# Between two transformer layers on one core: gated adds and residuals moved into TensorE's accumulators, row statistics read from PSUM, inverse roots by GpSimd's power

## What is computed

```python
h = layernorm(x) * (1 + ca) + sa
x = x + ga * L0_attn(h)            # adaptive window attention, 3 iterations, rows 0..308
h = layernorm(x) * (1 + cb) + sb
x = x + gb * L0_ffn(h)             # 8 experts, top 2 of softmax, gelu
h = layernorm(x) * (1 + ca1) + sa1
x = x + ga1 * L1_attn(h)           # W_in, complex decaying recurrence over tokens, W_out
h = layernorm(x) * (1 + cb1) + sb1
x = x + gb1 * L1_ffn(h)            # 8 experts, top 1, its own layernorm of h inside, relu
```

## Time and profile before

| | us |
|---|---|
| median of 3 runs | 447.66 (442.69 to 448.08) |
| profiled execution, span from first to last instruction | 450.3 |
| DVE busy in the span | 302.8 (67%) |
| PE busy | 299.0 (66%) |
| ACT busy | 171.9 (38%) |
| POOL busy | 171.5 (38%) |

### The profile page before, as it was taken

One profiled execution on the slowest core, in us unless ns is written; L12 is line 12 of the kernel. 1 busy time (PEld: TensorE's weight loads), 2 busy tenths in 40 slices (PEclk: granted clock), 3 DMA queues, 4 the chain that ended last, 5 costly groups with the idle time before them and its releaser, 6 DMA issues.

```text
span 450.3 us, 7419 instructions
## 1 busy us (share of the span) xinstructions
PE 299.0 (66%) x2070; PEld 218.3 (48%) x2071; DVE 302.8 (67%) x859; ACT 171.9 (38%) x331; POOL 171.5 (38%) x281
## 2 busy tenths in 40 slices
PE   2776888679916789786787999307616300599960
PEld 1662226333313232586687999303615300589960
DVE  7587975895779795288726666565988770277850
ACT  1144453216702157252515555747006600345520
POOL 9582870840166700002664455400000077044450
PEclk9885556555965557979989999856875555699995
DMA  2599700000011120011213221594000012323310
GB/s 78 97 366 362 229 3 0 1 1 1 8 47 41 53 32 0 1 34 51 60 48 72 64 66 38 157 307 146 1 1 1 0 59 106 97 69 81 97 48 0
DMA packets 37805, 32.93 MB, mean 73 GB/s; under 512 B 10765, under 2 KB 28770, under 8 KB 37776
## 3 DMA queue, kind: packets, MB, share of 16 engines
q1 hardware_dynamic: 33792, 25.10, 20.0%
q0 software_dynamic: 3936, 7.49, 5.3%
q10 hardware_dynamic: 48, 0.00, 0.0%
HBM read 19.50 MB, written 13.98 MB: 74 GB/s over the span
## 4 chain that ended last, share of the span: by engine, by line
PE 41%; DVE 30%; issue 10%; ACT 6%; POOL 5%; DMA 2%; DVEq 2%; SPq 1%; another core or an unknown queue 1%; POOLq 0%; ACTq 0%
PE ps L1237 9%; PE ps L1248 7%; PE ps L1058 6%; PE ps L1033 5%; PE ps L1053 5%; DVE mx L1765 4%; POOL rows L589 4%; DVE hb L1910 2%; DVE stats L1373 2%; PE ps L1009 2%; PE ps L1080 2%; ACT wide L782 2%; SPq L293 1%; POOL out L601 1%
## 5 line engine op out<-in xcount | busy, mean ns | idle before, releaser
L589 POOL DMA_INDIRECT rows<-token_rows,posu x48 | 49.1, 1024 | 115.1 <-DVE token_rows L1688 73.0
L601 POOL DMA_INDIRECT back<-ys,places x39 | 38.6, 990 | 81.9 <-DVE ys L1921 72.4
L1910 DVE TENSOR_TENSOR hb<-ps,b_in 128x512 f32<-128x512 f32 x62 | 42.5, 686 | 36.6 <-PE ps L1237 31.9
L1248 PE MATMUL ps<-w_out,hg 128*128 x496 | 66.3, 278 | 0.7 <-issue 0.7
L1248 PEld LDWEIGHTS ps<-w_out,hg 128*128 128x128 f32 x496 | 61.0, 194 | 1.1 <-issue 0.9
L871 ACT ACTIVATE hg<-hb 128x512 f32<-128x512 f32 x62 | 39.1, 630 | 36.4 <-DVE hb L1910 23.4
L1765 DVE TENSOR_REDUCE mx<-ps 128x2 f32<-128x512 f32 (+2 forms) x48 | 44.4, 948 | 7.2 <-PE ps L1033 6.6
L1237 PE MATMUL ps<-xsT,w_now 128*128 128x128 f32 x256 | 38.6, 299 | 10.8 <-DVE hb L1910 5.2
L1033 PE MATMUL ps<-feat,qs 64*128 64x281 bf16 (+2 forms) x128 | 33.3, 431 | 14.1 <-DVE mx L1765 10.0
L1237 PEld LDWEIGHTS ps<-xsT,w_now 128*128 128x128 f32 x256 | 34.6, 210 | 12.9 <-issue 8.4
L770 ACT COPY qs<-ps 128x768 bf16<-128x768 bf16 (+1 forms) x21 | 15.3, 728 | 64.4 <-PE ps L1009 38.8
(11 more groups left out here) (388 smaller groups left out, 549.6 us busy)
## 6 DMA issues: line engine op xcount, KB each, us to landing
rows<-blank SPq DMA_DIRECT2D x20, 260.0 KB, 7.3
xs<-rows SPq DMA_DIRECT2D x62, 64.0 KB
w_in<-in_L_ffn_w_fc SPq DMA_DIRECT2D x1, 2048.0 KB, 15.5
w_in<-in_L_ffn_W SPq DMA_DIRECT2D x1, 2048.0 KB, 10.2
rest<-rows SPq DMA_DIRECT2D x23, 65.0 KB
token_rows<-in_L_attn_x SPq DMA_DIRECT2D x1, 832.0 KB, 8.3
wmod<-in_L_wmod SPq DMA_DIRECT2D x2, 384.0 KB, 4.6
rows<-token_rows,posu POOLq DMA_INDIRECT x48
```

What stands on the lines that cost most here:

```text
L589: pool.indirect_dma_start(ROWS[l], bass.IndirectOffsetOnAxis(ap=posu[:, k, j:j + 1], axis=0), token_rows[:, j, 0:WIDTH[l]], None).then_inc ...
L601: pool.indirect_dma_start(where, bass.IndirectOffsetOnAxis(ap=target[r] if l else places[:, t, :].bitcast(U32)[:, 0:1], axis=0), ys[:, r, ...
L1248: mm = pe.matmul(ps[:, 6 + c % 2, 0:D], hg[:, c % RING, n * P:(n + 1) * P], w_out[:, bass.ds(e * NB + n, 1), :], start=(n == 0), stop=(n = ...
L1910: v.tensor_tensor(hb[:, c % 2, :].rearrange("p (b t) -> p b t", b=NB), ps[:, c % RING if h_bank(l, t) is None else h_bank(l, t), :].rearra ...
```

## The change

Everything is between the layers, but for one piece in layer 0's attention and one in the set-up. By part:

1. **Gates as diagonal matrices.** ACT writes, for each tile and each of the two experts, `identity * gate` (128x128): 26 for far tiles at the end of the third attention iteration, 6 for the near ones behind layer 0's experts. PE accumulates in PSUM, for each tile, `identity @ x + gate_matrix0 @ y0 + gate_matrix1 @ y1` (banks 0 to 3, in the order 3-6, 7-10, 11-14, 15 with 0-2). `gated` and `add_ffn` go.
2. **Statistics from PSUM.** DVE's bn_stats reads these banks; ACT's (for bank 3 DVE's) norm reads them too. ACT copies the sums back to x later.
3. **Roots by GpSimd.** For each bank or step POOL runs four small instructions: -mean, variance + eps, power -0.5, product. DVE's nine-instruction roots go, except one for tiles 7 to 15 behind the gates.
4. **Five steps behind the scan** (0-2, 3-6, 7-10, 11-14, 15). PE puts x first into the accumulator, W_out's products on top; DVE takes a step's sums between the scans of later steps.
5. **Modulation in the columns.** The second norm's 1 + cb and sb are applied by ACT on the way out of the transposition (scale and bias per partition); PE transposes the result back into PSUM (`turn_back`), where DVE takes the sums for the experts' layernorm and ACT norms into xn.
6. **Late part.** Steps 2 to 4 of that last layernorm come behind the choice and the gates; POOL scatters in five steps, each when its rows are there.

Some semaphores are merged and a table of -0.5 is set once.

```diff
+BANKS = [[3, 4, 5, 6], [7, 8, 9, 10], [11, 12, 13, 14], [15, 0, 1, 2]]
+STEPS = [(0, 3), (3, 7), (7, 11), (11, 15), (15, 16)]
 # POOL, in place of ready_to_send("all", 1) and 16 send_row
+            def scales(lo, hi, summed, done, value):
+                pool.wait_ge(sem(summed), value)
+                pool.tensor_scalar(minus_mean[:, lo:hi], mv[:, lo:hi, 0], -1.0, None, ALU.mult)...
+                then(pool.tensor_scalar(rstd[:, lo:hi], mv[:, lo:hi, 1], LN_EPS, None, ALU.add))
+                then(pool.tensor_tensor(rstd[:, lo:hi], rstd[:, lo:hi], minus_half[:, lo:hi], ALU.pow))
+                ins = pool.tensor_tensor(nmr[:, lo:hi], minus_mean[:, lo:hi], rstd[:, lo:hi], ALU.mult)
...
+            for b in range(len(BANKS)):
+                scales(4 * b, 4 * b + 4, "summed_a", "scaled_a", b + 1)
+            for c in range(len(STEPS)):
+                step_scales(c, "summed_1", "scaled_1")
+            for c in range(2):
+                step_scales(c, "summed_2", "scaled_2")
+            pool.wait_ge(sem("slots_all"), 1)
+            pool.wait_ge(sem("gates_all"), 1)
+            for c, (lo, hi) in enumerate(STEPS):
+                pool.wait_ge(sem("rows_all"), c + 1)
+                pool.wait_ge(sem("x_kept"), 5 + c)
+                for j in range(lo, hi):
+                    send_row("all", 1, 0, j)
 # ACT, attention, third iteration
                 take(2)
+                if it == 2:
+                    act.wait_ge(sem("gates_far"), 1)
+                    for j in range(NA, NA + 8):
+                        spread_gate(0, j)
                 take(3)
+                if it == 2:
+                    for k, j in [(0, j) for j in range(NA + 8, NT)] + [(1, j) for j in range(NA, NT)]:
+                        ins = spread_gate(k, j)
 # ACT, between the layers
+            bank_rows(0)
+            bank_rows(1)
+            turned_a(0)
+            bank_rows(2)
+            for b in range(1, 4):
+                turned_a(b)
+            keep(NT - 1, NT, ...); keep(0, NA, ...); for tiles in BANKS[:3]: keep(...)   # PSUM -> x
+            step_rows(0); keep_x(0); modulated(0)
+            step_rows(1); keep_x(1); modulated(1)
+            step_rows(2)
+            act.wait_ge(sem("scaled_1"), 5)
+            normalise(y0, range(*STEPS[4]), ...)
+            modulated(2); modulated(3); modulated(4); keep_x(2)
+            act.wait_ge(sem("rows1_dve"), 2)
+            keep_x(3); keep_x(4); step_sent(0)
             act.wait_ge(sem("lg_shifted"), 1)
             act.activation(lg2[:], lg2[:], ACT.Exp).then_inc(sem("lg_exp"), 1)
+            for c in range(1, len(STEPS)):
+                step_sent(c)
 # PE, between the layers
+            pe.wait_ge(sem("hb_ready"), T0)
+            for tiles in BANKS[:3]:
+                place_x(in_bank(tiles[0], tiles[0] + 4), tiles[0], tiles[0] + 4)
+            place_x(in_bank(NT - 1, NT), NT - 1, NT)
+            for b in range(3):
+                pe.wait_ge(sem(f"back_loaded{b}"), 32)
+                add_experts(BANKS[b]).then_inc(sem("added"), 1)
+            pe.wait_ge(sem("back_loaded3"), 32)
+            add_experts([NT - 1])
+            place_x(in_bank(0, NA), 0, NA)
+            turn_a(0)
+            pe.wait_ge(sem("back_loaded4"), 32)
+            add_experts(range(NA)).then_inc(sem("added"), 1)
+            modes_in(0)
+            for b in range(1, 4):
+                turn_a(b)
+                modes_in(b)
+            for c in range(4):
+                pe.wait_ge(sem("x_kept"), c + 1)
+                place_x(stepped(c, *STEPS[c]), *STEPS[c])
+            modes_out(0); modes_out(1); turn_f(0); modes_out(2); turn_back(0); turn_f(1)
+            modes_out(3); modes_out(4); turn_back(1)
+            logits(0); logits(1); turn_f(2); turn_f(3); turn_f(4)
+            logits(2); logits(3); logits(4).then_inc(sem("logits1"), 1)
+            for c in (2, 3, 4):
+                turn_back(c)
 # DVE, between the layers
+            for b in range(4):
+                bank_sums(b)
+            rotate_in(0)
+            v.wait_ge(sem("scaled_a"), 4)
+            for i, j in enumerate(BANKS[3]):
+                ins = v.tensor_scalar(xn[:, j, :], in_bank(j, j + 1), mean, root, ALU.subtract, ALU.mult)
+            for b in (1, 2, 3):
+                rotate_in(b)
+            scan(0); scan(1); step_sums(0); scan(2); step_sums(1); scan(3); scan(4)
+            step_sums(2); step_sums(3); step_sums(4)
+            v.wait_ge(sem("scaled_1"), 4)
+            (step 3's rows normed by tensor_scalar from PSUM)
+            for c in range(2):
+                sent_sums(c, ("summed_2", c + 1))
             read_logits("all") ... gates("all")
+            for c in (2, 3, 4):
+                sent_sums(c)
+            row_scales(4, 13)
+            for_scalar(4, 13, "scaled_2", 3)
```

More of the change, by code:

```diff
@@ L842, in _, with normalise @@
                 softmax_exp(it)
-            def normalise(dst, src, lo, hi, done):
-                for j in range(lo, hi):
-                    ins = act.activation(dst[:, j, :], src[:, j, :], ACT.Identity, scale=rstd[:, j:j + 1], bias=nmr[:, j:j + 1])
+            def normalise(dst, tiles, source, done):
+                for j in tiles:
+                    at = SLOT_OF[j]
+                    ins = act.activation(dst[:, j, :], source(j), ACT.Identity, scale=rstd[:, at:at + 1], bias=nmr[:, at:at + 1])
                 ins.then_inc(sem(done), 1)
@@ new lines, in add_experts, with turn_a @@
+            def add_experts(tiles):
+                for j in tiles:
+                    pe.matmul(in_bank(j, j + 1), gate_matrix(0, j), y0[:, j, :], start=False, stop=False)
+                    mm = pe.matmul(in_bank(j, j + 1), gate_matrix(1, j), y1[:, j, :], start=False, stop=(j == tiles[-1]))
+                return mm
+            def turn_a(b):
+                pe.wait_ge(sem("rows1a" if b < 3 else "rows1_dve"), b + 1 if b < 3 else 1)
+                if b >= 2:
+                    pe.wait_ge(sem("hT1"), b - 1)
+                for i, j in enumerate(BANKS[b]):
+                    mm = pe.transpose(ps[:, 4 + b % 2, i * P:(i + 1) * P], xn[:, j, :], ident[:])
+                mm.then_inc(sem("turned1"), 1)
@@ new lines, in logits @@
+            def logits(c):
+                pe.wait_ge(sem("hT1"), 4 + c + 1)
+                for j in range(*STEPS[c]):
+                    mm = pe.matmul(ps[:, 0, j * NE:(j + 1) * NE], hT[:, j * P:(j + 1) * P], wrl[:], start=True, stop=True)
+                return mm
+            modes_out(0)
+            modes_out(1)
+            turn_f(0)
+            modes_out(2)
+            turn_back(0)
+            turn_f(1)
+            modes_out(3)
+            modes_out(4)
+            turn_back(1)
@@ L1986, in _, with sums @@
             gates("near")
[L1988 to L1995 removed]
+            def sums(src, at, n, summed=None):
+                for i in range(n):
+                    ins = v.bn_stats(stats[:, at + i, :], src(i))
+                then(ins)
+                for i in range(n):
+                    ins = v.bn_aggr(mv[:, at + i, :], stats[:, at + i, :])
+                if summed:
+                    signal(ins, *summed)
+                else:
+                    then(ins)
```

342 lines of the change are left out of this document (198 added, 144 removed).

## The result

| | before | after |
|---|---|---|
| median | 446.13 us (442.69 to 448.08, 4 runs) | 427.39 us (425.67 to 431.35, 4 runs) |
| span of the profiled execution | 450.3 | 426.3 |
| PE, DVE, POOL busy | 299.0, 302.8, 171.5 | 312.2, 287.9, 193.4 |

The account below looks back on a forecast made before the run. The bound was a chain of waits between layers, 74.3 us with no engine full. Gates at 331 + 7.3 + 1.5 (port) + 0.5 (clock) = 340.3 instead of 360.9, 20.6 less: 447.7 - 20.6 = 427 us, range 418 to 439.

Parts of the forecast that it names:

- Part 1, cost 0: Layer 0's attention: ACT's 26 far gate matrices hidden, cost 0; at most 5.3 us if the cover fails.
- Part 2, the entry: Near gates to first scan: PE additions at 2.4 GHz, first scan at 306.0 instead of 316.2, a gain of 10.2 us.
- Part 3, the root: GpSimd's roots: power 0.6, root 1.6 us, four to five in series; bounds worth -1.8 and about +8.5 us.
- Part 4, order of waits: Scans to logits: sums 3 wait for W_out 3 behind step 1's turn; 25 us instead of 37.5.
- The 1.5 us for the port: Root 1 beside scan 3: contention with DVE delays turn 1 and W_out 3, 1.5 us added, bounds 0 and 2.6.
- The clock, 0.5: Between 300 and 320, PE about half idle: 0.5 us added for a clock that falls for a while.
- PSUM as source, 0: bn_stats and norms reading PSUM: change of source costed at 0; up to +1.2 us if 0.06 each.
- Part 5, hidden: Behind the logits: late sums and root hidden behind the gates with 2.9 us to spare; nothing changes behind the gates.
- (b): Rival: roots and hand-overs dearer, power at 2.4 us or POOL instructions behind DVE's; +8.5, 436 us; chance 0.20.
- (a): Rival: TensorE at 1.2 GHz from the entry on, gates near 357, gain 4, 443.5 us; chance 0.11.
- (c): Rival: GpSimd's power becomes the bound, 11 roots in a row; at 5.5 us a root +12, 460 us; chance 0.05.
- (d): Rival: cheap roots, no contention, full clock; gates at 335, 422 us; chance 0.64 together with the forecast.

Follow-up runs that it names:

- the four pairings of executions: The kernel before and the changed kernel, each profiled once more with nothing changed: 446.77 and 430.54 us, stages to the gates 73.89 and 56.43 us.
- doubling: A second power instruction into a spare tile in each of GpSimd's 11 roots, against the changed kernel: median 433.66 us, stage 4.9 to 6.1 us longer.
- the experiment: 16 unused matmuls in PE's pause between W_out 1 and turn 0, against the changed kernel: median 426.64 us, stage 1.0 to 2.1 us shorter.
- the repeated one: The changed kernel profiled once more, nothing changed: 430.54 us, stage to gates 56.43 us.

## Why the prediction was right, and what it owes to luck

The mechanism was forecast rightly, in order and for the most part in size, but that the number was hit to 0.4 us is luck. The stage came out 3 to 4 us longer than forecast (a gain of 16.6 in the two profiles, 16.3 to 17.8 over the four pairings of executions, where 20.6 were forecast). In the profiles that is 4.0 too little. Two things made up for it: a fourth run brought the kernel before from a median of 447.7 down to 446.1, worth 1.5, and the medians differ by 18.7, 2.1 more than the stage, which lies in layer 0 and chance. Step by step:

- **Part 1, cost 0**: right. Both covers held (ACT still waits 0.19 and 1.12 us behind them), with a ratio of 1.004 for this part alone.
- **Part 2, the entry**: order and clock (1.00 throughout) right. Counted from the near gates, banks 0 to 2 were added within 0.1 us of the forecast times, the near tiles 0.6 late. The first scan was forecast 19.6 us behind the near gates and came at 21.0, and the trace says where. ACT's rows 1 stand ahead of modulation 0 and wait for two roots, 0.35 to 0.4 longer each than my 1.6: W_in 0 began 0.7 late. Three rounds of 2.4 instead of 2.3 make 0.35, and the last W_in, 1.12 instead of 0.9, most of the rest.
- **Part 3, the root**: the mis-sized term. The power was taken at 0.6 and is 1.04, a root 1.95 instead of 1.6, well inside the two bounds (0.21 and 2.36). The number of roots in series, four to five, was about right (4.5 to 5.6 by doubling), with one more in the entry than forecast. Five times 0.35 is 1.7 us of the missing 3 to 4, the 0.7 of the entry included.
- **Part 4, order of waits**: right. Sums 3 waited for W_out 3 behind turn 1; scans took 13.4 us with their sums, as forecast. The wait for W_out 3 was 4.26 us where the forecast's times give 0.45 + 1.5: turn 1 was 0.6 late, counted from the first scan, and the clock (below) did the rest. The 1.5 us for the port was right for root 1 (1.71 measured), and without it the stage is 0.6 to 1.7 shorter. "Root 0 has slack" was wrong: it too lasts 3.5 us, turn 0 waited for it, and W_out 2 was queued behind turn 0. That this cost little (sums 2 only 0.4 us later against the first scan) is due to DVE's being busy with scans until 313.4.
- **The clock, 0.5**: too small. I saw that PE would be half idle but did not ask what stands first behind the longest pause. It fell within W_out 2 and stayed down through turn 1 (0.9 us instead of 0.45) and most of W_out 3 (3.2 instead of 1.8): 1.85 us more there, and 0.6 to 1.7 by the experiment.
- **Logits at 1.2 GHz, nine matmuls of 0.43**: right (18 records in 3.99), but not because of these matmuls, as I took it from the earlier trace rows: with the pauses ahead of them filled the 18 took 2.17. In the changed kernel the pause in front is 1.98 us.
- **PSUM as source, 0**: right. bn_stats takes 5 ns more for each tile than from SBUF. ACT's norm of four tiles takes 1.50 against 1.65 from SBUF.
- **Part 5, hidden**: right, both ways. In front of the logits it costs 5.1 to 6.2 us, and behind the gates GpSimd's 16 scatters followed one another without a wait. From the gates to the end 89.7 us went by, before and after, in the two profiles.

Some of the prediction's own signs went the wrong way and should be read with this. The power was to be under 1 us and is 1.04. Roots 0 and 1, at 3.50 and 3.66, are over the 3 us that stood as a sign of being wrong; beside scans this was rival (b)'s mechanism at two roots. DVE waited 3.71 and 2.26 us for banks 0 and 3, over the 2 that stood there too; the first of these waits is in the forecast's own times (bank 0 added 3.7 behind the near gates), so that sign was badly chosen. First scan and gates came at 300.0 and 336.8, not near 306 and 340, but the stage had begun 7.4 us earlier.

On the two rules that the prediction weighed. The Trainium skill, "SBUF — State Buffer", section "Who interferes with whom", has a VectorE instruction with two SBUF inputs and a GpSimd instruction that reads SBUF shut each other out: root 1 with and without scan 3 beside it agrees, 3.66 against 1.95. The Trainium skill, "VectorE: DVE Perf Modes", section "The TRN2 errata", gives 120 fixed cycles for a PSUM source against 58; by an estimate from this, four bn_stats from PSUM would have been 0.26 us longer. They were 0.02 longer, and the measurement decides.

Of the rivals, (a) did not occur: the clock stood at 1.00 through the entry, where PE's longest pause was 0.87 us; (c) needed a power of 4.4 us and met one of 1.04; (b)'s mechanism was there for roots 0 and 1, but its 8.5 us were not; (d) failed on the same numbers.

## What to carry to other kernels

An engine that works in written order makes everything behind a waiting instruction wait: here two turns, 0.4 and 0.9 us of work, held W_out, whose data was ready, and swapping them gave about 3 us. Before a root or any small chain goes to another engine, count it twice, its own length there and the room it leaves on the engine that it goes from; here the second was worth more. And a pause of TensorE can cost a second time in the work behind it (0.6 to 1.7 us here), so put what is ready into it, even work of no use if it ends in time.

## What the hardware showed that I had not expected

- GpSimd's power on fp32 takes 0.58 us for one column, 0.89 for three and 1.04 for four (128 partitions), so about 0.15 for each column on top of 0.43; its products and sums of that shape take 0.20 to 0.24.
- Three GpSimd instructions in a row beside a scan and its two rotations take 1.19, 0.71 and 1.32 us in place of 0.23, 0.23 and 1.04: each one is stretched, not only the first.
- Behind the same pause of 3.9 us the granted clock fell at different places. In the profiled execution the first matmuls of W_out 2 still ran at 0.225 us each (311.02 to 311.9) and those from 312.26 on at 0.43. In the repeated one it fell in the pause itself, near 313.6, with PE idle from 311.1 to 314.97, and turn 0 was slow already. With the pause filled it didn't fall there. With the roots on DVE it fell near 311.9, where PE's longest pause behind the first scan had been 2.18 us, so a pause of 3.9 us isn't needed for it.
- Layer 0, whose work was the same in all runs but for the gate matrices, ended anywhere from 274.3 to 286.4 us.
